# First attention's projections: tap weights made in the first stage, a norm step and the gates' tables moved, and no wait for the last stores

## The reference, cut to what matters

```python
x = x + 0.5 * _L0_ffn_ref(_layernorm(x), ...)          # stage 1, a top-1 FFN of 8 experts
x = x + _L0_attn_ref(_layernorm(x), ...)               # stage 2, the gated kernel attention
...
qkv = jnp.concatenate([x @ Wq, x @ Wk, x @ Wv], axis=-1)          # 1536 features
pad = jnp.pad(qkv, ((0, 0), (KW - 1, 0), (0, 0)))
conv = sum((pad[:, i:i + Tx, :] * Wconv[:, i] for i in range(KW))) # 4 taps along the tokens
qkv = jax.nn.silu(conv)
g = -jnp.exp(A_log) * jax.nn.softplus(x @ Wa + dt_bias)
alpha = jax.nn.sigmoid(x @ Walpha)
beta = jax.nn.sigmoid(x @ Wb)
k = k / (jnp.linalg.norm(k, axis=-1, keepdims=True) + EPS)
# then a scan over the tokens that carries two 64x64 states a head
```

## Time and profile before

| what | value |
|---|---|
| time, median of 3 runs | 2976.75 us (2976.27 to 2978.95) |
| time of the profiled execution | 2973.97 us |
| span of its trace | 2972.2 us |
| PE busy | 2751.4 us, 93% of the span |
| DVE, ACT, POOL busy | 1692.7, 1313.3, 364.2 us |
| stage 1, start to first instruction of stage 2 | 0 to 82.0 us |
| first part of stage 2 (projections) | 82.0 to 220.07 us |

### The profile page before, as it was taken

One profiled execution on the slowest core, in us unless ns is written; L12 is line 12 of the kernel. 1 busy time (PEld: TensorE's weight loads), 2 busy tenths in 40 slices (PEclk: granted clock), 3 DMA queues, 4 the chain that ended last, 5 costly groups with the idle time before them and its releaser, 6 DMA issues. The chain is left out here.

```text
span 2972.2 us, 36005 instructions
## 1 busy us (share of the span) xinstructions
PE 2751.4 (93%) x12273; PEld 1210.2 (41%) x12368; DVE 1692.7 (57%) x2737; ACT 1313.3 (44%) x2677; POOL 364.2 (12%) x413
## 2 busy tenths in 40 slices
PE   7878999988999799999999979999999879999888
PEld 3435666654444222222222224444444544444333
DVE  5667888864232788888888512333332433333565
ACT  3562333334454488888888854541110231111243
POOL 0324666620000500000000000000000000000000
PEclk9988999999999699999999999999999989999999
DMA  2243222211000311110200030022211012121000
GB/s 83 80 133 104 96 95 95 81 57 39 29 29 29 89 20 32 20 23 12 39 13 3 3 121 29 29 87 70 86 67 47 29 58 85 58 86 37 21 1 15
DMA packets 73308, 158.34 MB, mean 53 GB/s; under 512 B 12788, under 2 KB 44404, under 8 KB 70132
## 3 DMA queue, kind: packets, MB, share of 16 engines
q1 hardware_dynamic: 73164, 156.50, 17.0%
HBM read 137.40 MB, written 18.74 MB: 53 GB/s over the span
## 5 line engine op out<-in xcount | busy, mean ns | idle before, releaser
L2240 DVE TENSOR_REDUCE big<-psum 128x2 f32<-128x1024 f32 x512 | 603.5, 1220 | 77.5 <-PE psum L2069 73.6
L2202 ACT ACTIVATE probs<-psum 128x512 f32<-128x512 f32 x1024 | 553.1, 599 | 138.5 <-PE psum L2090 126.9
L2090 PE MATMUL psum<-big,k_ops 128*128 128x512 bf16 x945 | 294.8, 386 | 12.0 <-ACT probs L2202 6.8
L793 PE MATMUL psum<-xn,big 128*128 128x512 f32 x512 | 237.1, 603 | 9.4 <-ACT probs L853 7.2
L1005 PE MATMUL psum<-big 128*128 128x512 f32 x512 | 232.3, 605 | 11.7 <-DVE big L1136 11.7
L802 PE MATMUL psum<-probs,big 128*128 128x512 f32 x512 | 230.4, 594 | 0.0
L892 DVE SCALAR_TENSOR_TENSOR weighted<-psum,big 128x512 f32<-128x512 f32 x64 | 48.0, 751 | 316.4 <-PE psum L802 293.5
L1030 PE MATMUL psum<-probs,big 128*128 128x512 f32 x512 | 222.0, 593 | 4.6 <-issue 3.6
L1019 PE MATMUL psum<-big 128*128 128x512 f32 x512 | 224.5, 594 | 0.0
L2090 PEld LDWEIGHTS psum<-big,k_ops 128*128 128x128 bf16 x1024 | 81.3, 97 | 335.6 <-ACT probs L2202 260.1
L853 ACT ACTIVATE probs<-psum,big 128x512 f32<-128x512 f32 x256 | 171.9, 687 | 81.0 <-PE psum L793 75.2
(11 more groups left out here) (447 smaller groups left out, 3551.8 us busy)
## 6 DMA issues: line engine op xcount, KB each, us to landing
big<-row_store SPq DMA_DIRECT2D x128, 512.0 KB, 4.2
big<-step_rows SPq DMA_DIRECT2D x16, 1024.0 KB, 4.7
qkv_chunks<-big SPq DMA_DIRECT2D x48, 256.0 KB, 2.3
big<-qkv_chunks SPq DMA_DIRECT2D x16, 768.0 KB, 4.5
big<-since_rows SPq DMA_DIRECT2D x32, 256.0 KB, 5.2
big<-in_L SPq DMA_DIRECT2D x1, 6224.0 KB, 17.5
big<-in_L SPq DMA_DIRECT2D x1, 4197.0 KB, 13.3
big<-q_parts SPq DMA_DIRECT2D x27, 128.0 KB
```

Of the source, the lines that this page charges most:

```text
L793: pe.matmul(k.bank[3 + m % 3][:, :], w["we1"][:, e, c, :], xn[:, bass.ts(n, TB)], start=True, stop=True).then_inc(pre.sem, 1)
L2090: pe.matmul(k.bank[2 + m % 3][:, :], k_ops[:, g % 2, h, kt * P:(kt + 1) * P], q_ops[:, g % 2, i % QB, h, :], start=True, stop=True).then_i ...
L2202: act.activation(probs[:, kt % 2, h, :], k.bank[2 + m % 3][:, :], ACT.Exp, scale=SCALE).then_inc(expd.sem, 1)
L2240: dve.tensor_reduce(into, k.row_pair[hp].rearrange("p (h t) -> p h t", h=2), AX.X, ALU.max).then_inc(row_max.sem, 1)
```

## The change

It has five pieces.

1. The 16 products of `tap_w` move from POOL's start of stage 2 into `Opening.pool`, which is POOL's program in stage 1, behind the wait for the load of stage 2's weights and the tap rows (`loaded` at 32). `tap_w` gets a place of its own in `big`; other tiles are carved in another order so that nothing overlaps it. POOL's other preparations (a memset of 128x1536, four copies of the identity) move from the start of stage 2 to the end of block 0.
2. PE's `norm.pe_spread` moves from `j == 7` to `j == 9`, DVE's `norm.dve_norm` from `j == 8` to `j == 9`; `key_sums` moves from `j == 3` to `j == 1`, DVE's `sums` from `j == 5` to `j == 2`.
3. In the last block `act_logs` stands in front of `finish` of tile 0 instead of behind it, and the square root of the key sizes leaves it: it is taken in blocks 1 and 2 behind the layernorm's own square root. `pe_turn` moves from `j == 8` to `j == 7`, `act_steps` from 8 to 7, `dve_since` from 9 to 8.
4. SP stores the tables at `j == 8` and loads them (steps, since) and then the first chunk at `j == 9`. Before, it stored the tables and loaded the first chunk at `j == 10`, and loaded the tables at `j == 11`.
5. SP no longer waits for the last stores at the end of the part. ACT waits for them in the first chunk before it writes over their source (`wait_tiles` ahead of `o_copies`), SP at the end of its first chunk.

```diff
 class Opening:
@@ def pool
         self.cast(pool, "chunk_selector")
+        pool.wait_ge(self.k.loaded, 32)
+        self.taps(pool)
...
+def weighted_taps(k, w, pool):
+
+    for q in range(4):
+        for i in range(4):
+            pool.tensor_tensor(k.tap_w[:, q, i, :], w["proj"][:, 3 * q + 2, :], k.conv_rows[:, q, i, :], ALU.mult)
...
@@ GateTables
+    def wait_tiles(self, eng):
+
+        for kept in self.kept:
+            eng.wait_ge(kept.sem, kept.start + 16 * NB * 12 // 4)
+
+    def act_key_sizes(self, act, chunks):
+        act.activation(self.k_sum[:, chunks, :], self.k_sum[:, chunks, :], ACT.Sqrt)
...
@@ def act_logs
-        act.activation(k_sum, k_sum, ACT.Sqrt)
-        if i == 0:
+        if i == 1:
+            self.act_key_sizes(act, self.of(1))
+        else:
             act.activation(self.decay_rate[:, :], self.w["A_log"], ACT.Exp)
...
@@ project_and_convolve, PE
-                    if j == 3 and prev:
+                    if j == 1 and prev:
                         key_sums(n - 1)
...
-                    if j == 7 and nxt:
+                    if j == 9 and nxt:
                         norm.pe_spread(pe, n + 1)
-                    if j == 8 and not nxt:
+                    if j == 7 and not nxt:
                         gates.pe_turn(pe, 0, k.bank[0])
@@ ACT
                     copy(n, j)
+                    if j == 2 and not nxt:
+                        gates.act_logs(act, 0)
                     if j > 1:
                         finish(n, j - 2)
...
                         norm.act_deviation(act, n + 1)
-                    if j == 2 and not nxt:
-                        gates.act_logs(act, 0)
-                    if j == 8 and not nxt:
+                        if prev:
+                            act.wait_ge(sums_out.sem, sums_out.at(n - 1))
+                            gates.act_key_sizes(act, slice((n - 1) * TPB, n * TPB))
+                    if j == 7 and not nxt:
                         gates.act_steps(act, 0, k.bank[0])
@@ POOL
-            for q in range(4):
-                for i in range(4):
-                    pool.tensor_tensor(tap_w[:, q, i, :], w["proj"][:, 3 * q + 2, :], taps[:, q, i, :], ALU.mult)
...
-            pool.memset(tiles.state[0][:, :, :, :, :], 0.0)
...
+                if not prev:
+                    pool.memset(tiles.state[0][:, :, :, :, :], 0.0)
...
@@ DVE
-                    elif j == 5 and prev:
+                    elif j == 2 and prev:
                         sums(n - 1)
...
-                    elif j == 8 and nxt:
+                    elif j == 9 and nxt:
                         dve.tensor_scalar(ring[(n + 1) % 2][:, 0:3], ring[n % 2][:, TB:TB + 3], 0.0, None, ALU.add)
                         norm.dve_norm(dve, n + 1)
...
-                    elif j == 9 and not nxt:
+                    elif j == 8 and not nxt:
                         gates.dve_since(dve, 0)
@@ SP
-                    if n == NB - 1 and j == 10:
+                    if n == NB - 1 and j == 8:
                         gates.sp_keep(sp, 0)
+                    elif n == NB - 1 and j == 9:
+                        gates.sp_kept(sp, 0)
+                        tiles.load_steps(sp, 0, 0)
+                        tiles.load_since(sp, 0, 0)
                         for b in range(4):
                             sp.wait_ge(kept[b].sem, 16 * (NB - 1) * TILES // 4 + kept[b].start)
                         tiles.load_qkv(sp, 0, 0)
-                    elif n == NB - 1 and j == 11:
-                        gates.sp_kept(sp, 0)
-                        tiles.load_steps(sp, 0, 0)
-                        tiles.load_since(sp, 0, 0)
...
-            for b in range(4):
-                sp.wait_ge(kept[b].sem, 16 * NB * TILES // 4 + kept[b].start)
@@ run_chunks, ACT
+                if not prev:
+                    tables.wait_tiles(act)
                 o_copies(c, not nxt)
```

More of the change, by code:

```diff
@@ L468, with __init__ @@
 class Opening:
-    def __init__(self, k, here, weights_here, x_here, select_here, select, where, expert_b, bias_rest, casts):
+    def __init__(self, k, here, weights_here, x_here, select_here, select, where, expert_b, bias_rest, casts, taps):
+        self.taps = taps
         self.k, self.here, self.weights_here, self.x_here, self.select_here = k, here, weights_here, x_here, select_here
@@ L2333, in __init__ @@
         self.noughts = st("noughts", [P, CH])
+        self.kept = [k.counter(f"gka_kept_{b}") for b in range(4)]
         self.act_step, self.dve_step = k.counter("gka_act_step"), k.counter("gka_dve_step")
@@ L2351, in act_logs @@
     def act_logs(self, act, i):
-        z, tmp, k_sum = self.z[:, self.of(i), 16:36], self.tmp[:, self.of(i), :], self.k_sum[:, self.of(i), :]
+        z, tmp = self.z[:, self.of(i), 16:36], self.tmp[:, self.of(i), :]
         act.wait_ge(self.dve_step.sem, self.dve_step.at(3 * i))
-        act.activation(k_sum, k_sum, ACT.Sqrt)
-        if i == 0:
+        if i == 1:
+            self.act_key_sizes(act, self.of(1))
+        else:
             act.activation(self.decay_rate[:, :], self.w["A_log"], ACT.Exp)
@@ L2406, in passed @@
     def passed(self):
+        self.k.passed({f"gka_kept_{b}": 16 * NB * 12 // 4 for b in range(4)})
         self.k.passed({"gka_act_step": 4, "gka_dve_step": 6, "gka_steps_turned": 2, "gka_rows_kept": 64})
@@ L2417, in __init__ @@
         self.scores = [st(f"scores{b}", [P, G, R, CH]) for b in range(2)]
-        self.kd = st("kd", [P, PAIRS, R, 2, HD])
         self.o = st("o", [P, PAIRS, R, 2, HD])
@@ L2421, in __init__ @@
         self.oT = st("oT", [P, PAIRS * R, CH])
+        self.kd = st("kd", [P, PAIRS, R, 2, HD])
         self.x_new = st("x_new", [P, PAIRS, R, CH])
@@ L2461 @@
 GATES = 40
-PROJECT_WIDTH = 8900
+PROJECT_WIDTH = 9216
+TAPS_AT = PROJECT_WIDTH - 2048
+def weighted_taps(k, w, pool):
+    for q in range(4):
+        for i in range(4):
+            pool.tensor_tensor(k.tap_w[:, q, i, :], w["proj"][:, 3 * q + 2, :], k.conv_rows[:, q, i, :], ALU.mult)
 def project_and_convolve(k, w, scratch, gates, tiles):
@@ L2467, in project_and_convolve @@
     TILES, KTILE = 12, 8
-    st = Carve(k.big_high[:, 0:PROJECT_WIDTH])
+    st = Carve(k.big_high[:, 0:TAPS_AT])
     ring = [st(f"xn{b}", [P, 3 + TB]) for b in range(2)]
@@ L2474, in project_and_convolve @@
     acc = st("acc", [P, 2, TB])
-    tap_w = st("tap_w", [P, 4, 4, P])
-    taps = k.conv_rows
-    out = st("out", [P, 4, TB])
+    tap_w = k.tap_w
     halo = st("halo", [P, TILES, 4])
@@ L2480, in project_and_convolve @@
     k_sq = st("k_sq", [P, 2, TB])
+    out = st("out", [P, 4, TB])
     z, k_sum = gates.z, gates.k_sum
@@ L2596, in _ @@
             pool.memset(nought[:, :], 0.0)
-            for q in range(4):
-                for i in range(4):
-                    pool.tensor_tensor(tap_w[:, q, i, :], w["proj"][:, 3 * q + 2, :], taps[:, q, i, :], ALU.mult)
             pool.memset(ring[0][:, 0:3], 0.0)
             pool.drain().then_inc(taps_ready.sem, 1)
-            pool.memset(tiles.state[0][:, :, :, :, :], 0.0)
-            pool.memset(tiles.var_eps[:, :], 1e-6)
-            for r in range(4):
-                pool.tensor_copy(tiles.own_step[:, r, :], k.ident[:, :])
             def block_of(n, nxt, prev):
@@ L2621, in block_of @@
                                        ALU.mult).then_inc(squared.sem, 1)
+                if not prev:
+                    pool.memset(tiles.state[0][:, :, :, :, :], 0.0)
+                    pool.memset(tiles.var_eps[:, :], 1e-6)
+                    for r in range(4):
+                        pool.tensor_copy(tiles.own_step[:, r, :], k.ident[:, :])
             each_block(pool, block_of)
@@ L2684, in project_and_convolve @@
               "gka_haloed": NB * 8,
-              **{f"gka_kept_{b}": 16 * NB * TILES // 4 for b in range(4)}, "gka_k_squared": NB * 2, "gka_z_made": NB, "gka_z_out": NB,
+              "gka_k_squared": NB * 2, "gka_z_made": NB, "gka_z_out": NB,
               "gka_sums_made": NB, "gka_sums_out": NB})
@@ L2743, in chunk @@
                     tables.sp_kept(sp, 1)
+                    tables.wait_tiles(sp)
             each_chunk(sp, lambda: None, chunk, lambda: None)
@@ L3358, in build @@
         k.conv_rows = resident["conv_rows"].rearrange("p (q i c) -> p q i c", q=4, i=4)
+        k.tap_w = big[:, TAPS_AT:TAPS_AT + 2048].rearrange("p (q i c) -> p q i c", q=4, i=4)
         k.big_upper = big[:, 12500:24576]
@@ L3427, in build @@
         opening = Opening(k, here, weights_here, x_here, select_here, select, where["select"], piece("L0", "expert_b"), bias_rest,
-                          {"selector8": sel8, "selector16": sel16, "chunk_selector": selc})
+                          {"selector8": sel8, "selector16": sel16, "chunk_selector": selc}, lambda pool: weighted_taps(k, A0, pool))
         L0 = {n: piece("L0", n) for n in where["L0"]}
```

## The result

The changed kernel takes 2951.32 us (median of 4, 2949.27 to 2951.99) where the kernel before takes 2976.51 (median of 4): a ratio of 0.9914, 95% interval 0.9897 to 0.9931. It is 25.2 us faster; the forecast was 15.6 and its range ended at a gain of 22. In the later comparisons the kernel before stands at 2974.2 to 2975.1 us (medians of 7 to 31 runs), against which the same 2951.32 would be a gain of 23 to 24: part of the 25.2 is the first comparison's slower four runs. The profiled execution took 2949.27 us, with a span of 2947.5, 24.7 us under that of before.

A forecast was written before the change was run, and what follows sets the result against it. PE fills stage 1 (49.27 of 55.50 us) and most of a steady block (25.92 of 28.55), with idle gaps and a store wait. Terms sum to −15.6 us, 2976.75 to 2961.2 us; range 2954.5 to 2968.

The forecast's parts named there:

- taps in stage 1: Stage 1: POOL's tap products delay DVE's routing chain, for which PE waits; +2.3 us (0 to +6.7).
- So tile 9 gains less: Last block: after PE's idle of about 4 us and half clock, tile 9 gains some 2.2 us; 4.6 with full clock.
- the start: Start of the projections: taps are ready, PE goes on at once and DVE begins sooner; −6.8 us (−4.0 to −6.9).
- block 0: Block 0 of the projections: without the idle time PE keeps full clock; −0.9 us (0 to −1.5).
- blocks 1 and 2: Spread and norm at tile 9: PE's stall goes, but the norm delays tile 10; −0.3 us (0 to −5.2).
- last block: Last block: logs fill ACT's wait and table loads go, but PE idles before the turn; −2.6 us (−1 to −4.6).
- wait for the stores: End of the projections: SP no longer waits for its stores before the chunks; −7.3 us (−5.7 to −7.6).
- first chunk: First chunk: DVE's scan finds the steps loaded, and its scans cover the late q, k, v; 0 (−1 to +3).
- 11 of them are short ones: Stage 1: 11 short DVE operations beside the taps each lose half of 0.42 us, 2.3 us in all.
- the change does not do what it says: Rival, at the store wait: steps land as late as now, so the scan waits; within 6 us, chance 0.05.
- The POOL product that slowed DVE's first table step now slows a scan: no difference: First chunk: the slowdown by POOL's product moves from DVE's table step to a scan, at no gain or cost.
- The rival of a larger gain: Rival: taps miss DVE's chain, PE keeps its clock in the last block, norm frees 1 us a block; −22 us, chance 0.16.

The follow-up runs named there:

- norm undone: The changed kernel with PE's spread back at tile 7 and DVE's norm back at tile 8: 2955.05 us, ratio 0.9933.
- taps, no wait or gates alone: Three kernels, each the changed kernel with the other three pieces undone, keeping only taps' move, removed store wait or gates' steps: 2969.0, 2970.26, 2967.95 us.
- gates alone: The changed kernel with taps, norm and store wait put back, keeping the gates' steps, stores and loads of the last block: 2967.95 us, ratio 0.9979.
- norm alone: The changed kernel with taps, store wait and gates put back, keeping the spread and norm at tile 9: 2967.55 us, ratio 0.9981.
- the rest alone: The changed kernel with taps, norm, store wait and gates all put back; POOL's memset and copies, key sums and tile places stay changed: 2974.19 us, ratio 0.9999.
- Turn behind the taps: The changed kernel with PE's turn of the gates' table moved back to tile 8, behind that tile's tap products: 2950.95 us, ratio 0.9925.
- no wait alone: The changed kernel with taps, norm and gates put back, keeping only the removal of SP's wait for the last stores: 2970.26 us, ratio 0.999.

## Why the prediction fell short

The direction was right, and every place it named changed. Three steps of its sum failed: the 2.3 us for the taps in stage 1, the norm that was to take back what tile 9 gained (0.15 us a block), and in the last block "So tile 9 gains less". What follows the projections was put at nothing and brought 3.2 us. All these errors lie in one direction. Differences between the two profiled executions:

| term | forecast | measured |
|---|---|---|
| taps in stage 1 | +2.3 | +0.2 |
| the start | -6.8 | -6.8 |
| block 0 | -0.9 | -1.3 |
| blocks 1 and 2 | -0.3 | -2.0 |
| last block | -2.6 | -4.9 |
| wait for the stores | -7.3 | -6.7 |
| first chunk | 0 | -1.2 |
| second chunk and all behind it | 0 | -2.0 |
| sum | -15.6 | -24.7 |

*Taps in stage 1.* "11 of them are short ones", each losing half of 0.42 us, was too much: on the path six lose anything, 0.15 to 0.30 us each, 1.07 us together. That is the term mis-sized. That only 0.16 of it is left at L216 is in good part luck: PE's first rise to full clock came 0.8 us earlier in this execution than in that of before, and where the rises are equal 0.6 to 0.9 us are left. The prediction took stage 1 for full clock throughout and did not see the phase before 29.8. The Trainium skill, SBUF — State Buffer, section "SBUF: two separate sides", has only DVE operations with two SBUF inputs or in a two-port mode take part. The reductions at 0.19 us agree; the casts L303, with one input, are caught, as a two-port mode would be, though no run here shows their mode. Of the operations with two inputs not each is caught: L283 took 0.20 us beside the products, L294 0.49.

*Blocks 1 and 2, the step that failed in its mechanism.* It let tile 9 gain 1.1 us and tile 10 lose that again, with the norm "about 1.0 us with the columns". Counted from the block's first tile, tile 9 gains 1.3 us and tile 10 still 0.6. Tile 9 in fact follows tile 7 at once, and the norm with its columns puts 0.84 us between the end of tile 9 (133.28) and tile 10 (134.12), where 0.16 would stand without it; tile 10 then takes 0.35 us less beside POOL's squares. The period falls from 28.56 to 27.57 us. The same holds in block 0, where the term was not counted: norm undone costs 0.9 to 1.0 us in each of the three blocks that have a norm.

*A part that the profile of before could not show.* The spread's idle is a risk as well as a wait. Nine profiled kernels have the spread at tile 7. Four of them show a half-clock stretch behind it in both blocks 1 and 2, two in one, and three, the kernel before among them, in none. Seven have it at tile 9, and none shows one. A stretch costs 1.4 to 1.7 us. Of ten runs each, the kernels with taps, no wait or gates alone (spread at 7) range over 8.4 to 9.1 us and norm alone (spread at 9) over 4.9; but the rest alone, spread at 7 too, ranges over 5.8, so the ranges by themselves prove little. The stretches fit norm alone gaining 7.2 us where its trace shows some 4 to 5; that the unprofiled runs of before have such stretches is inferred, since they left no trace.

*Last block.* PE's idle of 4 us and its half clock came as forecast, 5.30 us for the taps. But "tile 9 gains less" did not follow: DVE was busy with the table and its scan until 189.61 and hid PE's delay. Counted from the block's first tile, tile 9 gains 3.3 us, not 2.2. Turn behind the taps removes the idle and gains nothing. Behind tile 9 another 1.6 came: DVE's scan no longer stands between tiles 9 and 10, and the last sums wait 0.75 us for PE, not 1.83. Of the 4.9, some 0.6 is this execution's short half-clock stretch; gates alone gains 4.2. The second SiLU table load "goes too" was wrong: the block has five table loads where it had six, and that one stands at 172.13, behind the logs.

*The wait and the first chunk.* Of the 7.3 us 6.7 came: SP's last store is issued at 197.56, beside the last sums, so that the meeting takes 1.12 us from them. The removed wait is worth its 6.7 us only because the steps are there; the rival "the change does not do what it says" is what no wait alone shows, with 4.25 us at the scan. Counted with that, the prediction's reason ("issued some 8 us sooner") was the right one. "The POOL product that slowed DVE's first table step now slows a scan: no difference" was half wrong. Before, POOL's two products slowed both that step (1.19 us for 0.29) and the first scan (2.02 for 1.2). Now they slow one scan, the fourth (2.23), so the 0.9 us at the step are saved.

*The rest of the program.* The forecast gave later stages no share. The half-clock stretch in the second chunk lasts 17.1 us (226.9 to 244.0) where it lasted 20.5 (248.2 to 268.7), and 0.95 us of the gain comes there; another 1.1 comes later in the program. The cause of both stays open.

The rival of a larger gain (-22 us, chance 0.16) came nearest in size, but of the three causes that "have to meet" only one came as stated, the norm's 1 us a block. The taps did not miss DVE's chain (1.07 us), and PE did not keep its clock in the last block (5.30 us for the taps): these two terms came out because other things hid the cost, an earlier rise of the clock and DVE's own work. As a forecast of the size 0.16 was too low; as an account of the causes the rival was wrong in two of three.

## What to carry to other kernels

Follow the engine that is the next bound, instruction by instruction, for both the gain and the price: here DVE's own work decided that PE's idle of 4 us cost nothing and that the norm's move paid in every block that has a norm. Two waits that stand beside each other, for stores and for loads, are priced together: one alone brought 4.5 us, the other 6.8, both 16.1. Where a short idle of PE stands in a loop, look in several traces at the granted clock behind it before its price is put at the idle alone. And where a difference of two traces crosses a change of the clock, compare traces in which it falls at the same moment.

## What the runs showed that was not expected

- The moment of PE's first rise to full clock moved between 27.3 and 31.0 us over 16 traces, with and without products on POOL beside the routing, and the end of stage 1 moved with it: it lies between 81.1 and 83.2 us in traces that have no half-clock stretch within it and no more products on POOL than the changed kernel.
- An idle of 2.5 to 2.6 us on PE is followed by 3.4 us at half clock in some executions and by none in others: ten of the eighteen blocks 1 and 2 in nine traces had such a stretch.
- A DVE scan of 128x512 that begins while POOL's product of 128x512 runs takes 2.0 to 2.2 us, and 1.2 us otherwise, in the first chunk of all 16 traces.
- A stretch of 3.4 us at half clock stands at 68 to 73 us, in the midst of stage 1, in five of the 16 traces, of kernels with and without the change, and costs about 1.7 us.
